# GNN kernel, aggregation stage: order of mixed sums, gates and square roots, four gate banks, and GpSimd's share of adds and splits

## The reference

```python
mean = s1 / safe;  mean_sq = s2 / safe
std = jnp.sqrt(jax.nn.relu(mean_sq - mean * mean) + 1e-05)
mn = jnp.where(has, segment_min(h, dst), 0.0)
mx = jnp.where(has, segment_max(h, dst), 0.0)
agg = jnp.concatenate([mean, mn, mx, std], axis=-1)
o1 = agg;  o2 = o1 * (logd / avg_log);  o3 = o2 * (avg_log / logd)
out = jnp.concatenate([m, o1, o2, o3], axis=-1) @ Wpost + bpost
gi = out @ Wih + bih;  gh = x @ Whh + bhh
r = sigmoid(ir + hr);  z = sigmoid(iz + hz);  n = tanh(i_n + r * h_n)
x2 = layernorm(x + (1.0 - z) * n + z * x)
```

## Time and profile before

| | before |
|---|---|
| median of three runs | 2864.03 us |
| lowest and highest run | 2863.81 and 2866.63 us |
| profiled execution, its own time | 2857.82 us |
| its span | 2856.0 us |
| busy TensorE / VectorE / ScalarE / GpSimd | 49% / 72% / 43% / 63% |
| mean granted clock of TensorE | 0.637 |
| the stage, from the loop's end to the last split | 2480 to 2578 us |

### The profile page before, as it was taken

The page is one execution under the profiler, slowest core; times in us unless marked ns, Lnnn a source line. Parts: engine busy times, 40 slices in busy tenths (PEclk is TensorE's granted clock), DMA queues, the critical chain, the costliest instruction groups (busy, mean ns, idle before and its releaser), DMA issues.

```text
span 2856.0 us, 29389 instructions
## 1 busy us (share of the span) xinstructions
PE 1404.1 (49%) x4582; PEld 607.2 (21%) x4583; DVE 2067.5 (72%) x3682; ACT 1215.1 (43%) x3258; POOL 1806.8 (63%) x1831
## 2 busy tenths in 40 slices
PE   2224555555544545334544444444434422388994
PEld 1101111111111111112311111111111100187552
DVE  6857777878856666677677888888767877844376
ACT  0013344344333333443355665666545545531222
POOL 3467777777777777773477777767777777203012
PEclk9996667666655666666555555555555555569997
DMA  5232222222222222221122222222222211108430
GB/s 139 58 80 59 57 58 62 57 58 60 52 62 59 61 63 62 63 63 28 49 59 59 59 60 63 58 56 66 50 59 59 56 30 30 48 1 292 146 112 7
DMA packets 124408, 187.02 MB, mean 65 GB/s; under 512 B 63129, under 2 KB 78958, under 8 KB 124186
## 3 DMA queue, kind: packets, MB, share of 16 engines
q0 software_dynamic: 57776, 89.59, 14.7%
q1 hardware_dynamic: 47598, 70.70, 7.9%
q10 hardware_dynamic: 18973, 26.03, 2.6%
HBM read 146.36 MB, written 39.84 MB: 65 GB/s over the span
## 4 chain that ended last, share of the span: by engine, by line
issue 15%; PE 12%; POOL 12%; DVE 7%; ACT 6%; DMA 3%; DVEq 2%; POOLq 2%; ACTq 0%
POOL arena L584 12%; ACT arena L1379 3%; PE mm L761 3%; DVE red L2136 3%; PE hist L991 2%; DMA arena<-b_tab,lin 2%; PE tp L991 2%; PE mm L913 2%; PE l L991 1%; PE l L1088 1%; PE tp L745 1%; DMA arena<-kv_tab,rec 1%; DMA rec<-rec_tab,win 1%; DVE arena L2159 1%; POOLq L677 1%
## 5 line engine op out<-in xcount | busy, mean ns | idle before, releaser
L584 POOL DMA_INDIRECT arena<-b_tab,lin x815 | 809.1, 993 | 290.2 <-issue 266.5
L584 POOL DMA_INDIRECT arena<-kv_tab,rec x815 | 810.6, 995 | 261.5 <-issue 236.9
L821 PE MATMUL l<-arena,identB 128*128 128x512 bf16 x996 | 389.7, 557 | 525.3 <-DVE arena L2012 516.5
L1379 ACT ACTIVATE arena<-arena,lin 128x64 f32<-128x64 f32 x1984 | 479.5, 333 | 0.0
L2136 DVE TENSOR_REDUCE red<-arena 128x128 f32<-128x2048 f32 x189 | 459.5, 2485 | 13.6 <-issue 12.8
L913 PE MATMUL mm<-Wshared,eaT 48*128 48x512 f32 x248 | 234.2, 1097 | 400.3 <-ACT eaT L1373 390.6
L2012 DVE TENSOR_SCALAR arena<-arena,digit 128x512 bf16<-128x512 int16 x744 | 257.3, 414 | 57.6 <-PE l L821 43.1
L843 PE MATMUL hist<-arena,oh_lo 125*128 125x225 bf16 x400 | 170.6, 583 | 235.5 <-DVE arena L1983 235.5
L821 PEld LDWEIGHTS l<-arena,identB 128*128 128x128 bf16 x996 | 114.7, 127 | 794.8 <-DVE arena L2012 618.7
L1376 ACT ACTIVATE arena<-arena 128x1024 f32<-128x1024 f32 x62 | 65.5, 1057 | 433.0 <-DVE arena L2159 433.0
L1298 ACT ACTIVATE arena<-T,digit,negdigit 128x512 bf16<-128x512 f32 x248 | 188.4, 806 | 8.6
(11 more groups left out here) (402 smaller groups left out, 2434.8 us busy)
## 6 DMA issues: line engine op xcount, KB each, us to landing
arena<-at_tab SPq DMA_DIRECT2D x50, 800.0 KB, 4.7
...
```

The lines of the kernel that those rows point to most:

```text
L584: return pool.indirect_dma_start(dst, None, table, offs(ap=index, axis=0))
L821: last = pe.matmul(l3[:, 0, :], identB[:], hot[:, j], start=False, stop=True, skip_group_check=True)
L1379: last = act.activation(dst[:, s], hh[u][:, s, 0:C], ACT.Identity, bias=bias[:, s:s + 1])
```

## The change

Eight edits, all in the stage or at its borders:

- VectorE adds the row term to the mean only; GpSimd adds it to the minimum and the maximum, third by third, and signals `extremes_added`. VectorE no longer waits for the square root; TensorE does, ahead of the second half of the transposes.
- TensorE makes all mixed sums ahead of all gates. Each step waits for the transposes of its own third only.
- The gates use four banks of their own (`l3` and `hist`), with the semaphores `gate_full` and `gate_used`.
- ScalarE loads the square root's table ahead of the edge loop and the sigmoid's ahead of the gates, each by an activation of one element that nobody reads. The square roots of the layernorm come behind all tanh, one for thirds 0 and 1 and one for third 2.
- VectorE makes states 0 and 1, then candidate 2 and state 2, and only then scales and splits: thirds 1 and 0 are scaled, 0 is split, 2 is scaled and split.
- GpSimd splits third 1 (`middle_set`, `middle_split`).
- The convolution starts with `FIRST` = 4 blocks, in three pieces: 8, 8 and 9 products each.
- SP loads tiles 3 and 4 behind the last `out_of` instead of behind `x_done`.

Left out of the diff below are declarations, and the places in `layers` where the numbers of `parts_ready` are one lower.

```diff
--- before.py
+++ after.py
@@ -369,14 +374,14 @@
 
         B_PARTS = [list(range(0, 8)), list(range(8, 12)), list(range(12, 20)), list(range(20, NB))]
         MM_AB = len(B_PARTS) + len(GROUPS)
-        MM_MLP = [2 + 2 * len(GROUPS) + 2 * len(PAIRS) + MM_AB, 2 + 4 * len(GROUPS) + 2 * len(PAIRS) + MM_AB]
+        MM_MLP = [2 + 2 * len(GROUPS) + len(PAIRS) + MM_AB, 2 + 4 * len(GROUPS) + len(PAIRS) + MM_AB]
         NG = len(GROUPS)
         LAG = 8
         CHUNKS = [GROUPS[0:2], GROUPS[2:4], GROUPS[4:]]
         CHUNK_PAIRS = [PAIRS[0:4], PAIRS[4:8], PAIRS[8:]]
-        MM_AGG = [MM_MLP[0] - 20 + k for k in (0, 2, 8)]
-        MM_GRU = [MM_MLP[0] - 20 + k for k in (4, 11, 15)]
-        FIRST = 3
+        MM_AGG = [MM_MLP[0] - 7 + k for k in (0, 2, 4)]
+        GATED = (0, 4, 8, len(PAIRS))
+        FIRST = 4
         tmin_small = at(26575, EP, 5, dt=I16)
         dst_next = at(26585, EP, 1, dt=I32)
         descents = at(26586, EP, 2)
@@ -408,6 +413,7 @@
                     in_bank[k] = (p, turn, side)
         scaled_by_act = lambda p, side: 2 * p + side + 1
         scaled_by_dve = lambda p, turn, side: 4 * p + 2 * (turn - 1) + side + 1 if 2 * p + 1 < NB else 4 * p + turn
+        gate_banks = [l3[:, 0], l3[:, 1], l3[:, 2], hist[:]]
         conv_banks = [[l3[:, 0], l3[:, 1], l3[:, 2], hist[:]], [hist[:], tp[:, 1]]]
         distance = [T1[:, GW * k:GW * (k + 1)] for k in range(2)]
         a_un = T1[:, 0:NP // 2].bitcast(BF16)
@@ -542,8 +548,8 @@
             big = sp.value_load(totI[0:1, 2:3], min_val=0, max_val=1)
             with sp.If(big < 1):
                 for s in range(2 * NB):
-                    if s == FIRST:
-                        sp.wait_ge(x_done, X2)
+                    if s == 3:
+                        sp.wait_ge(sums_done, OUT + 2)
                     if s >= 5:
                         sp.wait_ge(conv_full, s - 4)
                     dma(atL[s % 5], at_tab[s % NB]).then_inc(at_in[s % 5], 16)
@@ -692,6 +698,24 @@
                 gather_rows(2 * i - 1, 1, i, 2 * i)
                 gather_rows(2 * i, 0, i + 1, 2 * i + 1)
             gather_rows(2 * pairs - 1, 1, pairs, 2 * pairs)
+            pool.wait_ge(edges_counted, 1)
+            for c in range(3):
+                w = slice(CHUNKS[c][0][0], CHUNKS[c][-1][-1] + 1)
+                pool.tensor_tensor(agg[:, w, 1], accMn[:, w], xN[:, w], ALU.add)
+                pool.tensor_tensor(agg[:, w, 2], accMx[:, w], xN[:, w], ALU.add)
+                pool.drain().then_inc(extremes_added, 1)
+
+            pool.wait_ge(middle_set, 1)
+            w = slice(CHUNKS[1][0][0], CHUNKS[1][-1][-1] + 1)
+            pool.tensor_copy(parts2[:, w, 0], xN[:, w])
+            pool.drain()
+            pool.tensor_tensor(rest_mid[:], xN[:, w], parts2[:, w, 0], ALU.subtract)
+            pool.drain()
+            pool.tensor_copy(parts2[:, w, 1], rest_mid[:])
+            pool.drain()
+            pool.tensor_tensor(rest_mid[:], rest_mid[:], parts2[:, w, 1], ALU.subtract)
+            pool.drain()
+            pool.tensor_copy(parts2[:, w, 2], rest_mid[:]).then_inc(middle_split, 1)
             pool.wait_ge(x_done, X2)
             big = pool.value_load(totI[0:1, 2:3], min_val=0, max_val=1)
@@ -931,13 +955,15 @@
 
             def transpose_sums(c):
                 pe.wait_ge(sums_done, AGG + c)
+                pe.wait_ge(extremes_added, c + 1)
                 for h in range(2):
+                    if h:
+                        pe.wait_ge(act_r, SPREAD + c + 1)
                     for g in CHUNKS[c]:
                         transpose_group([agg[:, b, 2 * h:2 * h + 2].rearrange("p a c -> p (a c)") for b in g])
 
-            def mix_sums(c):
-                pe.wait_ge(tp_evac, ring["tp"])
-                pe.wait_ge(mm_evac, ring["mm"])
+            def mix_sums(c, copied):
+                pe.wait_ge(tp_evac, copied)
                 lo = CHUNKS[c][0][0]
                 for g in CHUNKS[c]:
                     product_group([(P, (P * j, P * (j + 1)),
@@ -950,31 +976,38 @@
                 for g in CHUNKS[c]:
                     transpose_group([sR[:, b] for b in g])
 
-            def gate_products(c):
-                pe.wait_ge(tp_evac, ring["tp"])
-                pe.wait_ge(mm_evac, ring["mm"])
-                for pair in CHUNK_PAIRS[c]:
-                    parts = []
-                    for j, b in enumerate(pair):
+            def gate_products(c, copied):
+                pe.wait_ge(tp_evac, copied)
+                for k in range(GATED[c], GATED[c + 1]):
+                    if k >= 4:
+                        pe.wait_ge(gate_used, k - 3)
+                    bank = gate_banks[k % 4]
+                    for j, b in enumerate(PAIRS[k]):
                         o = 4 * C * j
                         xb, ob = T2[0:C + 1, cols(b)], T1[0:C + 1, cols(b)]
-                        parts += [(P, (o, o + 2 * C), [(xb, Whh[:, 0:2 * C]), (ob, Wih[:, 0:2 * C])]),
-                                  (P, (o + 2 * C, o + 3 * C), [(ob, Wih[:, 2 * C:])]),
-                                  (P, (o + 3 * C, o + 4 * C), [(xb, Whh[:, 2 * C:])])]
-                    product_group(parts)
+                        pe.matmul(bank[:, o:o + 2 * C], xb, Whh[:, 0:2 * C], start=True, stop=False)
+                        pe.matmul(bank[:, o:o + 2 * C], ob, Wih[:, 0:2 * C], start=False, stop=True)
+                        pe.matmul(bank[:, o + 2 * C:o + 3 * C], ob, Wih[:, 2 * C:], start=True, stop=True)
+                        last = pe.matmul(bank[:, o + 3 * C:o + 4 * C], xb, Whh[:, 2 * C:], start=True, stop=True)
+                    last.then_inc(gate_full, 1)
 
             transpose_sums(0)
-            mix_sums(0)
+            mix_sums(0, ring["tp"])
             transpose_sums(1)
-            mix_sums(1)
+            mix_sums(1, ring["tp"])
+            transpose_sums(2)
+            summed = ring["tp"]
             transpose_out(0)
-            gate_products(0)
-            transpose_sums(2)
-            mix_sums(2)
+            outs = [ring["tp"]]
+            mix_sums(2, summed)
             transpose_out(1)
-            gate_products(1)
+            outs.append(ring["tp"])
+            gate_products(0, outs[0])
             transpose_out(2)
-            gate_products(2)
+            outs.append(ring["tp"])
+            gate_products(1, outs[1])
+            gate_products(2, outs[2])
+            pe.wait_ge(gate_used, len(PAIRS))
 
             def conv_begin(c, b):
                 n = NB * c + b
@@ -1092,11 +1125,14 @@
             def layers(conv):
 
                 if conv:
-                    pe.wait_ge(parts_ready, 2)
+                    pe.wait_ge(parts_ready, 1)
                     for b in range(FIRST):
                         conv_begin(0, b)
-                        conv_terms(0, b, 0, 16)
-                    pe.wait_ge(parts_ready, 3)
+                        conv_terms(0, b, 0, 8)
+                    pe.wait_ge(middle_split, 1)
+                    for b in range(FIRST):
+                        conv_terms(0, b, 8, 16)
+                    pe.wait_ge(parts_ready, 2)
                     for b in range(FIRST):
                         conv_terms(0, b, 16, NB)
                 for b in range(NB):
...
@@ -1389,6 +1425,7 @@
 
             asked()
             act.activation(S(LOGD_), S(LOGD_), ACT.Ln, bias=ones[:, 0:1]).then_inc(act_r, 1)
+            act.activation(unread[:], epsb[:], ACT.Sqrt)
             with aligned(act, 0, HI) as i:
                 for u in range(2):
                     step1(i, u, u == 0)
@@ -1414,14 +1451,13 @@
 
             def take_gates(c, first, last):
                 lo = CHUNKS[c][0][0]
-                for k in range(first, last):
-                    pair = CHUNK_PAIRS[c][k]
-                    bank = MM_GRU[c] + k
+                for k in range(GATED[c] + first, GATED[c] + last):
+                    pair = PAIRS[k]
                     b = slice(pair[0] - lo, pair[-1] + 1 - lo)
-                    v = mm[:, bank % 2].rearrange("p (b c) -> p b c", c=4 * C)[:, 0:len(pair)]
-                    act.wait_ge(mm_full, bank + 1)
+                    v = gate_banks[k % 4].rearrange("p (b c) -> p b c", c=4 * C)[:, 0:len(pair)]
+                    act.wait_ge(gate_full, k + 1)
                     act.activation(gates[c][:, b, 0:2 * C], v[:, :, 0:2 * C], ACT.Sigmoid)
-                    act.activation(gates[c][:, b, 2 * C:], v[:, :, 2 * C:], ACT.Copy).then_inc(mm_evac, 1)
+                    act.activation(gates[c][:, b, 2 * C:], v[:, :, 2 * C:], ACT.Copy).then_inc(gate_used, 1)
 
             def chunk_tanh(c):
                 s = slice(CHUNKS[c][0][0], CHUNKS[c][-1][-1] + 1)
@@ -1433,21 +1469,22 @@
             chunk_std(1)
             copy_sums(1)
             chunk_std(2)
+            copy_sums(2)
             copy_out(0)
+            act.activation(unread[:], epsb[:], ACT.Sigmoid)
+            copy_out(1)
             act.wait_ge(sums_done, AGG + 2)
+            act.wait_ge(extremes_added, 3)
```

(80 more changed lines are left out.)

15 lines of the change are left out of this document (10 added, 5 removed).

## The result

The changed kernel took 2857.14 us (median of 8 executions, 2854.35 to 2862.31) beside 2864.23 us before (8 executions, 2862.95 to 2866.63): ratio 0.9975, 95% interval 0.9964 to 0.9986. It is 7 us faster where 2 us slower was forecast. The sign was wrong, though the range held the time.

What follows compares the result with a forecast made beforehand. It took TensorE's gate products, paced by the granted clock, then VectorE's last state to bound the 98 us stage; +2.0 for later blocks, +0.4 for tile 5, -0.2 for banks gave +2.2 us, median 2866.3, range 2853 to 2874.

Steps and rivals of the forecast that it cites:

- how long the first gates keep the high clock: First third's gates on TensorE: 36 instructions in 4.1 us at 2.4 GHz, then 28 at the low clock, together 10.0 us.
- +2.0: Convolution start: four blocks done at 2586.8 instead of 2584.8, 2.0 us later in spite of 5.9 us won at the gates.
- rival 1: First sums and tail: GpSimd and VectorE hardly block each other; -7.9 us, 2856.1; chance 0.28 in whole or part.
- alternation: First sums and tail: GpSimd's work comes on top of VectorE's; 7.3 us for the adds, 4.5 for the split.
- The step to the median: Whole kernel: the profiled execution's +2.2 us difference carries over to the median, giving 2866.3 us.
- The two states behind the second gates: VectorE's candidates and states 0 and 1 end 15.8 us behind the second gates, just covered by the third gates.
- The 100 products of the four first blocks: Convolution start on TensorE: 30 instructions in 4.8 us, then 70 in 5.8, together 10.6 us.
- tile 5: Convolution loads: tile 5 starts only when block 0 ends and is waited for 0.4 us, up to 2.9.
- rival 2: Last third's transposes: pauses drop the clock, slowing mixed sums and gates; +8.8 us, 2875; chance 0.15.
- The tail's direction: Behind the last state: scaling and splits once hidden now show, so four blocks end later despite earlier gates.
- Rival 3: Edge loop on ScalarE: Square or Identity reload tables after the early square root; up to 40 us; chance 0.03.
- the four banks: Gate products on TensorE: four banks end its one wait for a bank, worth 0.2 to 0.3 us.

Runs made afterwards that it cites:

- the third of the changed kernel: The changed kernel run again unaltered, its profiled execution near the median; 2854.21 us, ratio 0.9980 to the kernel before.
- e3_early_tail: Against the changed kernel: each third scaled and split at once, earlier square roots back between the gates, VectorE splits the middle third, GpSimd's adds stay; 2847.84 us, ratio 0.9955.
- e8_banks_only: Against the kernel before: four gate banks, narrow waits, square-root wait at TensorE, table preloaded, four first blocks, earlier tiles; old order and tail; 2855.20 us, ratio 0.9986.

## Why the prediction failed, point by point

The steps of the prediction, in us behind T, with the profile of the changed kernel whose time is near its median:

| step | before | predicted | measured |
|---|---|---|---|
| second mixed sums start | 19.8 | 21.5 | 20.5 |
| gates start | 26.8 | 34.8 | 33.7 |
| gates end | 81.9 | 75.9 | 72.6 |
| last state made | 91.6 | 85.7 | 82.3 |
| first third split (`parts_ready` 1) | | 95.5 | 89.8 |
| products of four blocks done | 104.1 | 106.1 | 100.6 |

**What failed.** Two terms of the sum were mis-sized: how long the first gates keep the high clock, and what GpSimd's work costs VectorE beside it. By place they are 3.3 us up to the gates' end and 2.3 us in the tail, and together they turned +2.0 into -3.5.

*Gates, 3.3 us.* The second mixed sums did take 3.84 us, but they began 1.0 us sooner than forecast, since contention had taken less from VectorE. The gates kept the high clock for 6.2 us where I took 4.1 from the stretch before, which gave 57 fast instructions instead of 36: 21 times 0.098, 2.1 us. I had one row for how long the gates keep it, and made it a constant. The runs show it to vary: by the granted clock it is 5.7 to 6.6 us in the eleven profiles of the new order with narrow waits, 4.1 in the one with wide waits, and 2.7 to 4.2 where the gates come in the old order. So the term needed a range on the fast side, and the range's end in rival 1 (3 us further) should have stood with a chance of its own.

*Contention in the tail, 2.3 us.* The prediction laid GpSimd's split on top of VectorE's work (alternation, 4.5 us). From the last state to the split's end it took 7.5 us, not 9.8. GpSimd's split took 5.2 us as forecast (4.9), but VectorE paid only 2.2 for it, not 4.5: 0.16 on the multiply, 0.79 on each of two casts, 0.25 on each of two subtractions. At the start it paid 5.5 us for six adds (sums end at T + 18.9; they would have ended at T + 13.4), not 7.3. Alternation was the wrong model in size. An operation of GpSimd cost VectorE about 0.9 us of its 1.3 in the adds and under half in the split. Both engines move slower side by side (the add takes 2.25 us instead of 1.26, too).

*The step to the median.* The prediction carried the difference of the stage over to the median. Measured it is -3.5 us in the stage and -7.1 between the medians; the 3.6 us between them are the first open point below.

*A slip in a sum.* The two states behind the second gates come to 15.2 us by their own terms (1.6 and twice 6.8), not 15.8. Nothing hung on it: the last state followed the gates as forecast.

**What was right by its size.** The last state follows the gates by 9.7 us (9.8 forecast). The 100 products of the four first blocks take 10.7 us (10.6); tile 5 is waited for 0.3 us (0.4); the last third's mixed sums run at the high clock, so rival 2 fell. The tail's direction was right and is confirmed by two pairs of kernels: it costs 5.3 and 5.6 us, in both pairs without GpSimd's split, where the sum of the steps had 7.9 with it. Rival 3 fell: behind the square root ahead of the second edge loop, the next table load is the stage's own for the sigmoid, 1123 us later (timeline of the changed kernel, ScalarE, start and end of the loop):

```profile
1395.53 1.28 ACT L1428 ACT_TABLE_LOAD   x1
...
2518.51 1.28 ACT L1474 ACT_TABLE_LOAD   x1
```

In between lie the loop's 62 activations with Square and 1984 with Identity. By the rule of the Trainium skill that the prediction draws on (ScalarE: Activation LUTs, section "Table sets: the hidden batching unit") nothing would be reloaded for the loop's cheap functions, and the trace agrees; it shows the same for Square.

**Right for a wrong reason.** Rival 1 gave 2856.1 for the whole, 1 us from the median. Its mechanism isn't what happened: VectorE's operations beside GpSimd stand at 2.23 and 1.22 us, not at 1.36 and 0.43.

**A term I never wrote down.** I priced the four banks at 0.2 to 0.3 us and laid the gates and copies end to end, as if the waits' narrowing needed no price. It is a step of its own and as large as the order: with wide waits the new order lies 3.0 us below the kernel before, with narrow ones 9.9, so in the new order they are worth 6.9. The sum held it silently, so it did no harm to the forecast; it would have, had the waits stayed.

**Why faster and not level.** The banks, waits and four first blocks with the order bring some 10 us; the late tail takes 5.3 back; GpSimd's part brings nothing. That is 4.6 us, against 5.4 measured in the group that has most of these kernels, 7.1 and 9.9 in the two others.

**What stays open.** (1) The stage in the usual execution is 3.1 to 3.6 us shorter than in the profiles of before, and the medians are 5.4 to 9.9 apart. Either before's slower executions have a longer stage than its three profiled ones, or the rest lies ahead of T, which scatters from 2479.7 to 2486.8 us over the fourteen profiles of usual speed. A part of that scatter has a pattern. The stretch from the table load of a square root (at 1343.0 us before) to that of the logarithm (1388.9) lies ahead of the second edge loop. Five profiles (both of before, the third of the changed kernel, `e3_early_tail` and `e8_banks_only`) take 45.3 to 46.0 us for it, with the clock high until 1377 or 1378 us, and have T at 2479.7 to 2481.8. The nine others take 48.4 to 48.9 us, with the clock down by 1363 us, and have T at 2482.3 to 2486.8. So an execution can be 3 us slower by the clock in work that the change leaves alone, and both usual profiles of before had the fast course there. That speaks for a share ahead of T; it doesn't settle the size. (2) What GpSimd did in the 5.77 us.
